# Selective scan: one-hot rows built in layer 1's cross attention, weights loaded in layer 1's mixture, fills at the head of the inputs' block

## What is computed

```python
x = x + L1_xattn(layernorm(x), context)      # 16 heads, 64 context rows
x = x + L1_ffn(layernorm(x))                 # 8 experts, one chosen, capacity 256
x = x + L2_attn(layernorm(x))                # selective scan
```

```python
xz = x @ W_in.T;  xc, z = xz[..., :512], xz[..., 512:]
u  = silu(causal_conv(xc, conv_w) + conv_b)              # 4 taps, per channel
x_dbl = u @ W_x.T                                        # 1 step, 16 B, 16 C
dt = clip(softplus(x_dbl[..., :1] * W_dt + b_dt), 1e-4, 10)
A  = -exp(minimum(A_log, 5))                             # 16 states
h  = clip(h * exp(dt * A) + clip(dt * B * u, -10, 10), -100, 100)
y  = sum_n h * C
out = ((layernorm(y) * ln_g + ln_b) + D * u) * silu(z) @ W_out.T
```

## Time and profile before

| | us |
|---|---|
| median of 3 executions (2753.91 to 2758.6) | 2756.67 |
| the profiled execution, its own time | 2766.99 |
| its span, from the first to the last instruction | 2765.3 |

### The profile page before, as it was taken

The page is one execution under the profiler, slowest core; times in us unless marked ns, Lnnn a source line. Parts: engine busy times, 40 slices in busy tenths (PEclk is TensorE's granted clock), DMA queues, the critical chain, the costliest instruction groups (busy, mean ns, idle before and its releaser), DMA issues. The chain is left out here.

```text
span 2765.3 us, 28267 instructions
## 1 busy us (share of the span) xinstructions
PE 2137.1 (77%) x10151; PEld 1327.1 (48%) x10181; DVE 1714.5 (62%) x2529; ACT 1201.0 (43%) x1900; POOL 617.3 (22%) x349
## 2 busy tenths in 40 slices
PE   5688889595699979889473888888758979373894
PEld 3456556584223335668331444444535654252474
DVE  5554345424677745522464999999634776856665
ACT  2334322110276653311145899999713236302340
POOL 3321112120332101012114666564100210000100
PEclk8899799697899999879796999999869999696896
DMA  6553120243654300224200000000111000000001
GB/s 128 77 85 39 59 92 1 102 154 122 105 78 66 34 21 0 73 74 171 68 34 27 1 1 1 1 1 1 61 58 35 0 1 0 0 8 13 8 1 37
DMA packets 107529, 126.74 MB, mean 46 GB/s; under 512 B 14823, under 2 KB 98676, under 8 KB 106357
## 3 DMA queue, kind: packets, MB, share of 16 engines
q1 hardware_dynamic: 94404, 109.63, 17.7%
q10 hardware_dynamic: 10098, 7.71, 0.9%
q0 software_dynamic: 2880, 7.48, 0.7%
HBM read 91.11 MB, written 33.29 MB: 45 GB/s over the span
## 5 line engine op out<-in xcount | busy, mean ns | idle before, releaser
L3148 DVE TENSOR_TENSOR_SCAN l2s_h<-l2s_aw 128x2048 f32<-128x2048 f32 x64 | 290.0, 4532 | 5.2 <-ACT l2s_rs L3193 5.2
L3107 PE MATMUL l2s_big<-g_xn,g_ident 128*128 128x512 f32 x512 | 259.0, 608 | 11.5 <-ACT g_xn L3186 6.4
L3162 POOL TENSOR_SCALAR l2s_aw<-l2s_aw 128x2048 f32<-128x2048 f32 x64 | 211.0, 3298 | 10.3 <-DVE l2s_aw L3140 5.1
L582 DVE TENSOR_REDUCE l1at_nm<-l1at_s 128x1 f32<-128x512 f32 x256 | 162.2, 683 | 66.7 <-PE l1at_s L432 65.7
L3099 PE MATMUL l2s_c_ps<-g_ident,l2s_h 128*128 128x128 f32 x1024 | 148.9, 279 | 55.7 <-ACT g_xn L3186 37.0
L3099 PEld LDWEIGHTS l2s_c_ps<-g_ident,l2s_h 128*128 128x128 f32 x1024 | 117.3, 141 | 146.4 <-issue 86.7
L680 ACT ACTIVATE g_xn<-l1at_s 128x512 f32<-128x512 f32 x256 | 143.4, 598 | 82.2 <-PE l1at_s L456 81.7
L3186 ACT ACTIVATE g_xn<-l2s_c_ps,l2s_ct 128x512 f32<-128x512 f32 x256 | 163.0, 690 | 17.1 <-PE l2s_c_ps L3099 16.9
L582 DVE TENSOR_REDUCE l0at_nm<-l0at_s 128x2 f32<-128x384 f32 x128 | 70.0, 557 | 101.0 <-PE l0at_s L432 99.9
L3179 ACT ACTIVATE l2s_aw<-l2s_dt,l2s_A 128x2048 f32<-128x2048 f32 x64 | 128.3, 2006 | 0.0
L3107 PEld LDWEIGHTS l2s_big<-g_xn,g_ident 128*128 128x128 f32 x512 | 82.0, 190 | 81.8 <-ACT g_xn L3186 58.6
(11 more groups left out here) (882 smaller groups left out, 4879.5 us busy)
## 6 DMA issues: line engine op xcount, KB each, us to landing
l1f_w<-in_L_ffn_w_dram SPq DMA_DIRECT2D x16, 1024.0 KB
l0f_w<-L_ffn_experts_inter_dram SPq DMA_DIRECT2D x7, 1024.0 KB
l0f_w<-n_L_ffn_experts_out_dram SPq DMA_DIRECT2D x7, 1024.0 KB
l0at_qs<-l0at_parts SPq DMA_DIRECT2D x18, 256.0 KB
l0at_ks<-l0at_parts SPq DMA_DIRECT2D x18, 256.0 KB
l1at_qs<-l1at_parts SPq DMA_DIRECT2D x18, 256.0 KB
l1at_ks<-l1at_parts SPq DMA_DIRECT2D x18, 256.0 KB
expert_rows<-g_zeros SPq DMA_DIRECT2D x1, 4096.0 KB, 13.7
```

The source lines that it names most:

```text
L582: V.tensor_reduce(nm[:, s % 2, qts[0]:qts[-1] + 1, r], s1[:, u % 3, 0:len(qts) * KEYS].rearrange("p (q k) -> p q k", k=KEYS), AX, ALU.max, ...
L3107: nc.tensor.matmul(acc[:, tb, :], ident[:], hCT[:, tb, :], start=n == 0, stop=n == NST - 1).then_inc(acc_done, 1)
L3148: V.tensor_tensor_scan(out=h_all[:, i % 2].rearrange("p c t -> p (c t)"), data0=dA[:, i % 2].rearrange("p c t -> p (c t)"), data1=wd[:, i ...
L3162: nc.gpsimd.tensor_scalar(wd[:, i % 3], wd[:, i % 3], 10.0, -10.0, ALU.min, ALU.max).then_inc(clipped, 1)
```

## The change

It does four things.

1. The tensors `aw` (the scan's work buffer), `sel`, `cols`, `conv_w` and `A` and two semaphores move to a new object, `ScanParts`, in a new scope `l2w` that is open from l1x to the end of the scan. A scope marked `holder` does not take over the semaphores of the scopes in it, so l1x, l1f and l2s are cleared and meet at a barrier when they end, as before, and `l2w` does so once more at its own end. The weights' raw copies are now parts of `aw`.
2. GpSimd builds `sel` in l1x's second block.
3. SyncE issues all 12 loads in l1f's experts' block, between the weights of the last expert and the wait for the expert rows, and waits for them at the end of that block. `prepare` gets an empty list of loads.
4. The scan's second and third block are gone. VectorE's program of `scan_inputs` begins with `clear`: `A`'s first step, the clearing of `hmax`, `rs` (GpSimd's before) and `xd3`, and `A`'s last step. ScalarE's begins with `A`'s exponential.

```diff
@@ class Scope
+        if len(self.opened) > 1 and not self.opened[-1].holder:
             self.opened[-1].sems += self.sems
         elif self.sems:
             self.nc.clear_and_free_semaphores(self.sems)
             self.nc.all_engine_barrier()
@@ narrow_cross_attention, second block
         with S.block() as block:
+            if scan is not None:
+                @block.gpsimd
+                def _(pool):
+                    scan.make_rows(pool)
@@ mixture, the experts' block, SyncE
                     weights(sp, e)
+                if scan is not None:
+                    scan.load(sp)
                 for u in range(2):
                     sp.wait_ge(put[u], 16 * CTL * len(range(u, n_exp, 2)))
...
+                if scan is not None:
+                    scan.wait_loaded(sp)
@@ new
+class ScanParts:
+    def __init__(self, nc, S, wts):
...
+        self.aw = S.sb("aw", [P, 5, self.C4, SEQ])
+        self.sel = S.sb("sel", [P, 2 * self.NST, P], BF16)
...
+        flat = [self.aw[:, n].rearrange("p c t -> p (c t)") for n in range(3)]
+        self.raw_in = flat[0].rearrange("p (t d) -> p t d", d=DM)
+        self.raw_out = flat[1][:, 0:KC * self.DI].rearrange("p (k d) -> p k d", d=self.DI)
+        self.raw_x = flat[2][0:self.NX, 0:self.DI]
+
+    def make_rows(self, pool):
+        sel, nst = self.sel, self.NST
+        ch = Chain(pool, self.made)
+        ch.step(self.nc.gpsimd.memset(sel[:], 0.0))
+        for n in range(3):
+            ch.step(self.nc.gpsimd.affine_select(out=sel[:], in_=sel[:], compare_op=ALU.not_equal, fill=1.0, base=-2 * nst * n,
+                                                 pattern=[[-1, 2 * nst], [0, P]], channel_multiplier=1))
+
+    def load(self, sp):
...
+            for dst, src in loads:
+                sp.dma_start(dst, src).then_inc(self.loaded, 16)
+        self.loads = 16 * len(loads)
+
+    def wait_loaded(self, sp):
+        sp.wait_ge(self.loaded, self.loads)
@@ selective_scan
-            with nc.allow_non_contiguous_dma(reason="per-channel vectors"):
-                prepare(nc, name + "t", c, loads, jobs)
-            with R.block() as block:
...
+        prepare(nc, name + "t", c, [], jobs)
...
-        with S.block() as block:
-            @block.vector
-            def _(dve):
-                nc.vector.memset(T["xd3"][:], 0.0)
-
-            @block.gpsimd
-            def _(pool):
-                nc.gpsimd.memset(T["rs"][:], 0.0)
@@ scan_inputs, VectorE
+            def clear():
+                V.tensor_scalar(A[:], A[:], 5.0, None, ALU.min).then_inc(a_ready, 1)
+                V.memset(hmax[:], 0.0)
+                V.memset(T["rs"][:], 0.0)
+                V.memset(xd3[:], 0.0)
+                dve.wait_ge(a_ready, 2)
+                V.tensor_scalar(A[:], A[:], -1.0, None, ALU.mult)
+
             def program():
+                if not exact:
+                    clear()
                 convolve(0)
@@ scan_inputs, ScalarE
             def program():
+                if not exact:
+                    act.wait_ge(a_ready, 1)
+                    E.activation(A[:], A[:], ACT.Exp).then_inc(a_ready, 1)
                 for m in range(C4):
                     channels(0, m)
```

More of the change, by code:

```diff
@@ L3551, in decoder_kernel, with _ @@
             self_attention(nc, "l1at", c, of("L1_attn_"), given=True, window=False)
-        if stage(4):
-            c["norm"] = ("l1b", None)
-            narrow_cross_attention(nc, "l1x", c, of("L1_xattn_"), out_in=True)
-        if stage(5):
-            c["norm"] = ("l1c", None)
-            mixture(nc, "l1f", c, of("L1_ffn_"), 8, 1, c["moe1"])
-        if stage(6):
-            c["norm"] = ("l2a", None)
-            selective_scan(nc, "l2s", c, of("L2_attn_"))
+        with Scope(nc, "l2w", holder=True) as S6:
+            parts = ScanParts(nc, S6, of("L2_attn_")) if stage(6) else None
+            if stage(4):
+                c["norm"] = ("l1b", None)
+                narrow_cross_attention(nc, "l1x", c, of("L1_xattn_"), out_in=True, scan=parts)
+            if stage(5):
+                c["norm"] = ("l1c", None)
+                mixture(nc, "l1f", c, of("L1_ffn_"), 8, 1, c["moe1"], scan=parts)
+            if stage(6):
+                if first >= 5:
+                    with S6.block() as block:
+                        @block.gpsimd
+                        def _(pool):
+                            parts.make_rows(pool)
+                        @block.sync
+                        def _(sp):
+                            if first == 6:
+                                parts.load(sp)
+                                parts.wait_loaded(sp)
+                c["norm"] = ("l2a", None)
+                selective_scan(nc, "l2s", c, parts)
         with Scope(nc, "l2q") as S8:
```

73 lines of the change are left out of this document (29 added, 44 removed).

## The result

| | kernel before | changed kernel |
|---|---|---|
| median of 4 executions, us | 2757.64 (2753.91 to 2762.83) | 2738.86 (2738.17 to 2740.34) |
| ratio, 95% interval | | 0.9929 [0.9914, 0.9945] |
| the profiled execution, its own time, us | 2766.99 | 2739.08 |
| its span, us | 2765.3 | 2737.4 |
| mean granted clock | 0.884 | 0.885 |

What follows compares the result with a forecast made beforehand. The prediction took the chain at the scan's head, with nothing needed later running beside it, as the bound. 2.6 + 17.4 + 1.4 - 0.7 = 20.7 us off the median 2756.67 gives 2736.0 us, range 2732 to 2743.5.

Steps and rivals of the forecast that it cites:

- layer norm's block without its loads: Layer norm ahead of the scan: TensorE turns 16 weight blocks beside the statistics, last copy of `xn` 2.6 us earlier.
- end of the norm to the projection: Scan's head: two blocks go, one change of block of 0.3 us stays; gain 17.4 us, 17.1 to 17.5.
- projection to first convolution: Head of `scan_inputs`: 3.5 us becomes 2.1, TensorE at 2.4 GHz, VectorE's `clear` setting the time; gain 1.4 us.
- loads in the mixture: Layer 1's mixture: 12 issues stand in SyncE's idle stretch behind the last expert's weights; cost 0.
- `sel` in l1x: l1x's second block: VectorE's instructions take PSUM operands, so GpSimd's 15.3 us don't hold it; cost 0, other end 15.3.
- one more scope's end: Scan's end: one more clearing of two semaphores costs 0.7 us, between 0.5 and 1.4.
- The condition on the clock: Layer norm's block: the 2.6 us gain holds if TensorE's groups of `xn` come at 2.4 GHz from the third on.
- half clock: Rival: TensorE at 1.2 GHz through the layer norm's block and first projection; gain 17.5 us, 2739.2; chance 0.18.
- The half-clock price of 3.5 us: Head of `scan_inputs`: at 1.2 GHz the first channel takes its 3.5 us again, gain 0.
- The forecast's second argument: Mixture: even with all loads' work ahead of them, the last expert's weights would land at 1322.8, just before use at 1323.20.
- the last of the signs by which the prediction would have been wrong: Scan: the time between the first convolution and the end of the scan is not what it was.

Runs made afterwards that it cites:

- second profile of before: Kernel before, unchanged, run again against itself: ratio 0.9997, span 2759.6 us.
- early rows: Changed kernel, but GpSimd builds `sel` in the cross attention's first block, ahead of its addition to x: 2747.86 us in one execution.
- the loads put first: Changed kernel, but SyncE issues the 12 loads ahead of the last expert's two weight loads: 2743.12 us in one execution.
- the rows three times: Changed kernel, but GpSimd's four instructions for `sel` are made three times in a row in l1x's second block: 2741.87 us in one execution.
- rows alone: Changed kernel, but GpSimd builds `sel` in a block of its own between the layer norm and the inputs' block: ratio to before 0.9994.
- fills alone: Changed kernel with the two blocks of fills and exponential back, `sel` staying in l1x: ratio to before 0.9953, second run 0.9951.
- third profile of the changed kernel: Changed kernel, unchanged, a third time, on one chip with the kernels with loads or fills put back: ratio to before 0.9932.
- loads back: Changed kernel, but the 12 loads stay in the layer norm's block, half on SyncE, half on ScalarE: ratio to before 0.9944, second run 0.9949.
- weights first: Changed kernel, but ScalarE copies the turned weights before its root and takes six of eight groups of `xn`: ratio to before 0.9942.

## Why the prediction was right, step by step

Differences are from profile to profile of the two kernels, us.

| term | forecast | measured |
|---|---|---|
| layer norm's block without its loads | -2.6 | -2.9 (-3.7 from the second profile of before) |
| end of the norm to the projection | -17.4 | -17.4 (17.70 to 0.32) |
| projection to first convolution | -1.4 | -1.5 (3.51 to 2.00; -1.8 from the second) |
| loads in the mixture | 0 | 0 |
| `sel` in l1x | 0 | 0 |
| one more scope's end | +0.7 | +0.4 |
| sum | -20.7 | -21.4 (-22.4 from the second) |

**The layer norm's block** went as its steps said. Counted from the block's opening, ScalarE's first copy was forecast at 7.3 us and came at 7.2, the weights' last copy at 11.9 and 11.7, TensorE's `xn` at 10.6 and 10.4, VectorE's last copy at 16.3 and 16.0. The condition on the clock held: it rose 11.5 us after the opening, during `xn`. That was in part luck. The block's program is the same in the kernels with `sel` or the loads moved, and in three of their six profiles the clock rose later: 14.7 us after the opening with early rows, where the block took 16.96 us; at 14.1 with the loads put first (16.65) and at 13.7 with the rows three times (16.49), after it had risen and fallen once before the second burst of weights. So half clock cost up to 1.0 us here, though in none of the three profiles of the changed kernel, which all took 15.96. The forecast's 1.8 for it (2.6 against 0.8) was for a clock that never comes back.

**The two blocks** were the largest term and the surest, since nothing runs beside them and only the length of a change of block was open. The single parts, taken back one at a time, don't add up to it: rows alone are worth 15.9 us before the projection and fills alone 3.4, in sum 19.3, but 17.4 together, because in the kernel before the first block's fills lie beside `sel`.

**The head of `scan_inputs`.** Clearing cost 0.17, 0.17, 0.48 and 0.91 us where 0.17, 0.17, 0.46 and 0.91 were forecast, and the convolution began 2.00 us after the projection (2.1). The half-clock price of 3.5 us that the forecast set against this was itself from a start in which the clock came back in time: with the clock down for the whole first channel it is 3.8 us, in the second profile of before and in the kernels with a block put back. The minimum of `A`, 3.36 us beside GpSimd's clearing, is 0.17 us with GpSimd idle.

**The loads** cost nothing, but the reason was half wrong: "about 0.6 us each, 7 us". SyncE needed 14.6 us, one issue alone 4.10, with the DMA engines 0.85 to 1.09 busy from 1306 to 1318; a window of it in the changed kernel (columns as above, the DMA share being last but one):

```profile
1310.00:1314.00 4.00, 3.81 (x21) 3.16 (x20) 1.47 (x3) 0.47 (x1) 0.00 (x0) 1.00 1.08 381
```

In the layer norm's block of the kernel before, with no expert's weights under way, an issue took 0.4 to 1.1 us (ScalarE's six, from 1356.70 to 1361.07), which is the price that I had used. With 22 us to spare behind the weights it did not matter. The forecast's second argument, that the weights would land just before their use even with all 12 loads ahead of them, was wrong: put in that order, they landed 1.5 us too late.

**`sel` in l1x.** The argument went from one product with a PSUM operand in the scan to all of l1x's second block, and held; l1x took 142.3 us, but so it did in an execution of the kernel before, and 141.0 in the third profile of the changed kernel.

**The scope's end** was 1.84 - 1.43 = 0.41 us of VectorE's idle time and not 0.7.

```profile
2008.30 4.42 DVE L2745 TENSOR_TENSOR g_x<-g_x,g_xn 128x4096 f32<-128x4096 f32 x1 [11.86 <-PEq L3386]
2014.56 2.71 DVE L1021 BATCH_NORM_STATS2 l2xp_st<-g_x 128x6 f32<-128x256 f32 x8 [1.84 <-PEq L55]
```

The idle time ahead of the first of these two rows, where the flag is looked at, was 13.26 us in the first profile of before and lies between 11.7 and 12.9 in all others. That scatter is the 1.4 us by which the scan's part (-22.8) exceeds the sum.

**The time.** 2738.86 against 2736.0 is within the scatter of a median: the three ratios of the changed kernel are 0.9929, 0.9918 and 0.9932, and 21.4 to 22.4 us of 2760 would be 0.9922 to 0.9919, which the intervals of all three hold.

From the first convolution to the closing's first statistics it is 569.4 us in the kernel before and 569.3 in the changed one, so the last of the signs by which the prediction would have been wrong did not appear either.

## What to carry to other kernels

Work that nobody waits for in one part (constants, weights of the next part, clearing) can go where its engine idles in an earlier one, and the price is read there: what shares its port in that block, and what is queued behind it on its queue. A short block between two parts costs its own length and also the clock of TensorE behind it: 3.4 us of blocks cost 5.2 here. Even a part that the change does touch has more than one length in the kernel before (the head, 40.06 and 41.11 us), so a forecast from one profile carries that scatter. Before an effect of 5 us is believed from two profiles, compare the parts that the change does not touch.

## What the hardware showed that was not expected

- TensorE's clock stayed at 1.2 GHz for the first 6.0 us of gapless transposes in one execution (loads back, first run) and rose 2.9 us into them in another of nearly the same program. In the other two with these loads it rose after 5.5 us.
- It fell in idle gaps of 3.69 us (weights first) and 4.55 us (fills back), and not in the gap of about 1 us ahead of the changed kernel's projection.
- Issuing a DMA from SyncE took up to 4.10 us while the DMA engines were 0.85 busy and the last expert's weights were under way. The same issue with the loads put first, before those weights, took 0.58 us.
- l3s took 95.4 to 95.8 or 100.5 to 100.9 us at two levels of the clock, from execution to execution of one kernel. What selects the level isn't known from these runs.
